# Two-layer graph network: the four table blocks of the 512-wide layer become 44, 45, 47 and 48

## The chip, the cores and the metric

The kernel runs as one program on one core of a Trainium2 chip. The metric is the device time of a run in microseconds, the median of several runs. Of the engines, PE does the matmuls, DVE and ACT elementwise work, POOL the indirect gathers, and SP and ACT issue plain DMAs.

## What is computed

A graph of 6250 nodes and 100000 edges, sorted by destination, passes through an attention layer with batch norms and a feed-forward part, and then three aggregations of the same kind over the same edges:

```python
def _gin_conv(h, src, dst, w, b, eps, n_nodes):
    agg = jax.ops.segment_sum(h[src], dst, num_segments=n_nodes)
    return ((1.0 + eps) * h + agg) @ w + b
...
h = jax.nn.relu(_gin_conv(x, src, dst, w1, b1, eps1, n))   # 256 -> 512
h = jax.nn.relu(_gin_conv(h, src, dst, w2, b2, eps2, n))   # 512 -> 512
return _gin_conv(h, src, dst, w3, b3, eps3, n)             # 512 -> 256
```

The kernel moves the weights around the sum, so that the first and the third aggregation run on rows of 256 values and the second on rows of 512. Each gathered row is `h[src]` of an edge, and the sum goes to the edge's destination.

## The kernel before

The 6250 destination nodes are 50 blocks of 125 (`BLOCKS`, `NB`). The sum of a block is made in one of two ways. A gathered block reads its edge records (up to `RE` = 2176 in a round of `T` = 17 times 128), POOL issues 17 indirect gathers of 128 source rows, DVE makes 17 one-hot matrices, and PE multiplies them. A table block uses a dense count table in DRAM: `adjacency[b]` holds, for each of the 50 source blocks, how many edges run from each source node to each node of block b (128 x 6250 bf16, 1562.5 KB), and PE multiplies table parts with source rows. Edges of a block whose lists overflowed would be gathered in small rounds of `OV` = 32; each table block has at least one such round, on padding.

The stages run one after another, with a barrier between them:

- Edge records and lists are prepared.
- The build (L479 to L616) makes the tables of the blocks in `BUILT`, in rising order. For each of 25 groups of five nodes DVE compares a list with two iotas (L569 `low_hot`, L570 `code_hot`), PE multiplies the two (L615), and 13 evictions per table, on ACT (L587) and from table 12 on one of them on DVE (L567), write a stage buffer that SP stores (L537). From table 12 on POOL does 10 of the 25 `low_hot` comparisons (L522, `low_aside`). Two stage buffers alternate by the table's place d in `BUILT`.
- Attention, batch norms, feed-forward.
- `mixed_layer(0)`, the first 256-wide layer: blocks with b modulo 3 equal to 1 are gathered (L1828), the 33 others (`DENSE_BLOCKS`) use tables, loaded by ACT in parts (L1935).
- `wide_layer(1)`, the 512-wide layer: 46 blocks are gathered (L2258) and four are table blocks. Their sums are kept in four PSUM banks all through the layer; for each of the 50 source blocks, beside the gathers, `source_sums` (L2471) adds that source's contribution to all four. `load_parts` (L2379) fetches the piece of the four tables that belongs to four source blocks, `cast_source` (L2391, L2393) makes it ready, `split_source` (L2321) splits the source rows. The four tables are read with one DMA, through a rearranged view with every second block. `part_loaded` counts these loads. Only in the last eight steps is a block's number a constant; before them it is 2i + s in a loop.
- `mixed_layer(2)`, the last layer, from `rows_last`, which the 512-wide layer has filled by block.

ACT's order in a step of the 512-wide layer: `copy_turned` (the tile `l_zT`, L2361), `store` (L2368), `keep_upper`, then `cast_source` with its loads. The layer begins with six to eight source steps before and around the first gathered block.

Of the kernel before, what the change touches and what calls it, by code (L numbers as in the profile page):

```python
# [57 lines left out]
GATHERED_AT = 1  # L58
TABLED_BLOCKS = [BLOCKS - 2 * TABLED + 1 + 2 * d for d in range(TABLED)]
DENSE_BLOCKS = [b for b in range(BLOCKS) if b % PERIOD != GATHERED_AT]  # L60
BUILT = sorted({*DENSE_BLOCKS, *TABLED_BLOCKS})
DENSE = len(BUILT)
# [35 lines left out]
def build(nc, x, src, dst, Wq, bq, Wk, bk, Wv, bv, Wo, bo, W1, b1, W2, b2, g1, be1, g2, be2,  # L98
# [12 lines left out]
    with ExitStack() as ctx:  # L111
# [1962 lines left out]
        def wide_layer(n, table, w):  # L2074
            k_tiles = w // P
            with ExitStack() as phase:
# [43 lines left out]
                def tabled(s, i):  # L2120

                    return s == 1 and isinstance(i, int) and i >= PAIRS - TABLED

                def record_of(s, i):

                    return (i - (PAIRS - TABLED)) % 2 if isinstance(i, int) and i >= PAIRS - TABLED else s
# [35 lines left out]
                def edge_range(engine, s, i):  # L2162

                    b = 2 * i + s
                    if tabled(s, i):
                        ends = [dense_ends[0:1, e, bass.ds(b, 1)] for e in range(2)]
                    else:
                        ends = [first_edge[0:1, bass.ds(b + e, 1)] for e in range(2)]
                    lo, hi = [engine.value_load(end, min_val=0, max_val=E) for end in ends]
                    return lo, hi  # L2170
# [19 lines left out]
                def _(sp):  # L2190
# [9 lines left out]
                    def load_block(s, i):  # L2200
                        lo, hi = edge_range(sp, s, i)
                        if tabled(s, i):
                            load_few(lo, hi)
                        else:
                            t = record_of(s, i)
                            with sp.Fori(lo, hi, RE) as at:

                                sp.wait_ge(round_gathered[t], count_of(sp, rounds[t]) + 1)
                                sp.dma_start(record[t][:, :, :].rearrange("p j c -> p (j c)"),
                                             edges[bass.ds(at, RE), :].rearrange("(p j) c -> p (j c)", j=T)).then_inc(record_loaded[t], 16)  # L2210
                                sp.reg_add(rounds[t], rounds[t], 1)
                        sp.wait_ge(own_used[s], i + 1)
                        sp.dma_start(own[s][:, :], block_rows(table, 2 * i + s)).then_inc(own_loaded[s], 16)

# [57 lines left out]
                def _(dve):  # L2272
# [9 lines left out]
                    def onehot_few(s, i, lo, hi):  # L2282
                        with dve.Fori(lo, hi, OV) as at:
# [3 lines left out]
                            order.step(dve.tensor_scalar(few_relative[:, :], few_record[:, 1:2].bitcast(F32),  # L2287
                                                         minus_base[0:OV, bass.ds(2 * i + s, 1)], None, ALU.add))
                            dve.tensor_scalar(few_onehot[:, :], column[0:OV, 0:NB], few_relative[:, :], None,
# [4 lines left out]
                    def rounds_of(s, i):  # L2294
# [5 lines left out]
                        with dve.Fori(lo, hi, RE) as at:  # L2300
                            before = count_of(dve, rounds[t])
                            dve.wait_ge(record_loaded[t], before * 16 + 16)
                            order.step(dve.tensor_scalar(relative[t][:, :], record[t][:, :, 1].bitcast(F32),
                                                         minus_base[:, bass.ds(2 * i + s, 1)], None, ALU.add))
                            dve.wait_ge(quarters_used, count_of(dve, seen[t]) * NQ + NQ)
# [35 lines left out]
                    def halve(s, i):  # L2341
# [3 lines left out]
                        dve.sem_inc(upper_cut[s], 1)  # L2345
                        dve.tensor_tensor(rows_last[:, bass.ds(2 * i + s, 1), D:2 * D].rearrange("p o c -> p (o c)"), result[s][:, :],
                                          upper[s][:, :], ALU.subtract).then_inc(lower_ready[s], 1)
# [5 lines left out]
                def _(act):  # L2353
# [10 lines left out]
                    def store(s, i):  # L2364
                        act.wait_ge(product[s], i + 1)
                        act.wait_ge(lower_ready[s], i + 1)
                        act.wait_ge(stored[s], (i + 1) * 16)
                        act.activation(result[s][:, :], product_ps[0:NB, 0:D], ACT.Copy).then_inc(result_ready[s], 1)  # L2368
                        act.wait_ge(result_ready[s], i + 2)
                        act.dma_start(block_rows(table3, 2 * i + s), result[s][:, :]).then_inc(stored[s], 16)  # L2370

                    def keep_upper(s, i):
                        act.wait_ge(upper_cut[s], i + 1)
                        act.activation(rows_last[:, bass.ds(2 * i + s, 1), 0:D].rearrange("p o c -> p (o c)"), upper[s][:, :],
                                       ACT.Copy).then_inc(upper_ready[s], 1)

                    def load_parts(u):
                        width = min(4, BLOCKS - 4 * u) * NB if isinstance(u, int) else 4 * NB
                        act.dma_start(packed[:, :, 0:width],  # L2379
                                      adjacency.rearrange("(d k) p x -> k p d x", k=2)[1, :, PAIRS - TABLED:PAIRS, bass.ds(u * (4 * NB), width)]  # L2380
                                      ).then_inc(part_loaded, 16)

# [3 lines left out]
                    def cast_source(r, a, u):  # L2386

                        v = u * 2 + a // 2
                        act.wait_ge(part_loaded, u * 16 + 16)
                        act.wait_ge(source_used[r], v + 1)  # L2390
# [132 lines left out]
```

## Time and profile before

| | |
|---|---|
| median of 3 runs | 4995.4 us (4991.88 to 4999.53) |
| span of the profiled execution | 4893.1 us |
| around the span, median less span | 102.3 us |
| busy: PE, DVE, ACT, POOL | 78%, 46%, 29%, 55% of the span |
| DMA, mean over the span | 150 GB/s |
| table stores | 35, 1562.5 KB each |
| loads of 500 KB (part loads of the 512-wide layer) | 12, and a smaller thirteenth |

The shares are means over stages that have different limits, so the trace is read by stage: the busy times of a stretch say which engine is never idle, and the timeline of a line that runs once per table or per block gives the pace. An idle time stands in brackets behind an instruction, with what ended it; "issue" means that the trace shows nothing that the engine waited for. SPq and ACTq rows are issues of DMAs on those queues, not their transfers.

### The profile page before, as it was taken

Reading aid. Unit: us, or ns where it says so; the run is one execution under the profiler, and the core shown is the slowest. Engines: PE = TensorE matmul, PEld = TensorE weight load, DVE = VectorE, ACT = ScalarE, POOL = GpSimd, SP = SyncE. Lnnn points to the kernel's source line nnn. Section 1 sums busy time; section 2 is a strip of 40 time slices with the busy share of each in tenths; the row PEclk is TensorE's granted clock in tenths of the full one; section 3 lists DMA queues with packets and bytes.
Section 4 is the critical chain, followed back from the end, with each engine's and each line's share of the span. In section 5 each row is a group of like instructions: output and inputs, shape, how many; then the busy total and the mean of one; then the engine's idle time right before and its main releaser. Section 6 shows DMA issues by size and latency. Waiting matters only on the chain. (4 is left out here: it accounts for less than half of the span.)

```text
span 4893.1 us, 71187 instructions
## 1 busy us (share of the span) xinstructions
PE 3799.9 (78%) x15901; PEld 2488.7 (51%) x15902; DVE 2235.7 (46%) x7891; ACT 1434.7 (29%) x2745; POOL 2679.8 (55%) x4185
## 2 busy tenths in 40 slices
PE   3886645656566556986999999688888888779999
PEld 1233324444444444875677777344444444457777
DVE  6997756767676677345121121222222222222222
ACT  3983222222222222245344444100000000023333
POOL 6781056676766666013544444266666666646664
PEclk9999977777777777985999999799998999889999
DMA  4442233333333333026767666477777776646665
GB/s 138 176 184 92 58 82 92 95 97 96 96 96 96 94 96 86 0 67 179 201 183 206 189 183 185 138 211 210 214 210 206 209 214 206 197 135 208 204 202 178
DMA packets 346846, 734.87 MB, mean 150 GB/s; under 512 B 77407, under 2 KB 171229, under 8 KB 341985
## 3 DMA queue, kind: packets, MB, share of 16 engines
q0 software_dynamic: 176144, 461.72, 33.4%
q10 hardware_dynamic: 100178, 157.63, 10.3%
q1 hardware_dynamic: 70268, 113.00, 6.7%
q14 instruction: 204, 1.67, 0.1%
q8 instruction: 52, 0.85, 0.1%
HBM read 622.28 MB, written 109.84 MB: 150 GB/s over the span
## 5 line engine op out<-in xcount | busy, mean ns | idle before, releaser
L900 POOL DMA_INDIRECT a_gathered<-table,record x850 | 808.2, 951 | 642.6 <-issue 378.5
L2258 POOL DMA_INDIRECT l_gathered<-table,record x782 | 761.0, 973 | 472.1 <-issue 283.4
L2451 PE MATMUL bank<-l_gathered,l_onehot 128*125 128x512 f32 x1564 | 777.0, 652 | 179.1 <-DMA l_gathered<-table,record 110.7
L1828 POOL DMA_INDIRECT l_gathered<-table,record x578 | 546.1, 945 | 463.4 <-PE bank L2036 215.9
L1249 PE MATMUL bank<-a_gathered,a_onehot 128*125 128x264 f32 x1700 | 570.3, 494 | 101.6 <-DVE a_gathered L1053 79.0
L2451 PEld LDWEIGHTS bank<-l_gathered,l_onehot 128*125 128x125 f32 x1564 | 316.3, 207 | 617.3 <-issue 457.6
L1942 ACT ACTIVATE l_part<-l_packed 128x1000 fp32r<-128x1000 bf16 (+1 forms) x396 | 413.3, 1070 | 554.4 <-PE bank L2017 227.1
L1249 PEld LDWEIGHTS bank<-a_gathered,a_onehot 128*125 128x125 f32 x1700 | 393.5, 243 | 203.9 <-issue 76.5
L2017 PE MATMUL bank<-rows_first,l_part 125*125 125x512 f32 x1650 | 406.6, 405 | 29.3 <-ACT l_part L1942 29.2
L2017 PE MATMUL bank<-rows_last,l_part 125*125 125x512 f32 x1650 | 394.5, 398 | 11.3 <-ACT l_part L1942 9.9
L2017 PEld LDWEIGHTS bank<-rows_first,l_part 125*125 125x125 f32 x1650 | 308.4, 187 | 121.2 <-issue 43.9
L2017 PEld LDWEIGHTS bank<-rows_last,l_part 125*125 125x125 f32 x1650 | 304.3, 186 | 89.2 <-issue 12.1
L615 PE MATMUL bank<-d_code_hot,d_low_hot 128*128 128x250 bf16 x875 | 268.7, 385 | 49.7 <-DVE d_code_hot L570 24.2
L587 ACT ACTIVATE d_stage<-bank 128x500 bf16<-128x500 f32 (+1 forms) x432 | 285.5, 726 | 34.9 <-PE bank L615 27.1
L1053 DVE TENSOR_TENSOR a_gathered<-a_gathered,bank 128x1024 f32<-128x1024 f32 x200 | 244.0, 1282 | 40.6 <-ACT bank L1192 27.8
L1892 DVE SCALAR_TENSOR_TENSOR l_work<-rows_first,one_eps,bank 125x256 f32<-125x256 f32 x50 | 24.0, 481 | 497.2 <-PE bank L2044 464.6
L570 DVE TENSOR_SCALAR d_code_hot<-d_code_iota,d_lists 128x250 bf16<-128x250 bf16 x875 | 247.2, 318 | 0.0
L2361 ACT ACTIVATE l_zT<-bank 128x500 f32<-128x500 f32 x50 | 29.3, 587 | 737.0 <-issue 491.7
L2036 PE MATMUL bank<-l_gathered,l_onehot 128*125 128x256 f32 (+1 forms) x867 | 210.7, 400 | 17.1 <-DMA l_gathered<-table,record 17.0
L615 PEld LDWEIGHTS bank<-d_code_hot,d_low_hot 128*128 128x128 bf16 x875 | 91.0, 104 | 226.6 <-DVE d_code_hot L570 79.1
L1264 PE MATMUL bank<-identity_bf,a_onehot_bf 128*128 128x128 bf16 x850 | 82.5, 236 | 144.9 <-ACT a_onehotT L1175 68.5
L569 DVE TENSOR_SCALAR d_low_hot<-d_low_iota,d_lists 128x128 bf16<-128x128 bf16 x645 | 193.7, 303 | 1.2 <-ACT d_lists L577 1.2
(282 smaller groups left out, 5515.3 us busy)
## 6 DMA issues: line engine op xcount, KB each, us to landing
l_packed<-adjacency ACTq DMA_DIRECT2D x265, 250.0 KB
adjacency<-d_stage SPq DMA_DIRECT2D x35, 1562.5 KB
l_packed<-adjacency ACTq DMA_DIRECT2D x132, 281.2 KB
l_gathered<-table,record POOLq DMA_INDIRECT x1360
a_gathered<-table,record POOLq DMA_INDIRECT x850
table<-rows_first POOLq DMA_DIRECT2D x50, 250.0 KB, 3.5
table<-l_work ACTq DMA_DIRECT2D x50, 250.0 KB
l_source_rows<-table ACTq DMA_DIRECT2D x50, 250.0 KB
```

The costliest lines, as they stand in the source:

```text
L570: dve.tensor_scalar(code_hot[g % HOT][:, :], code_iota[:, :], lists[:, c, 1, k:k + 1], None, ALU.is_equal).then_inc(pair_ready, 1)
L587: act.activation(*evict(d, h), ACT.Copy).then_inc(summed_read, 1)
L615: pe.matmul(banks[n % 7][:, (g - g0) * CODES:(g - g0 + 1) * CODES], low_hot[at % HOT][:, :], code_hot[at % HOT][:, :], start=True, stop=Tr ...
L900: pool.indirect_dma_start(out=gathered0[s][:, j * TW:(j + 1) * TW], out_offset=None, in_=table0, in_offset=bass.IndirectOffsetOnAxis(ap=re ...
L1053: dve.tensor_tensor(values[:, j0:j1], values[:, j0:j1], factors[:, j0:j1, :].unsqueeze(3).broadcast_to([P, j1 - j0, HEADS, DH]), ALU.mult) ...
L1249: last = pe.matmul(acc_ps[s][0:NB, 0:TW], onehot[s][:, j, :], rows[:, j, :], start=(j == 0), stop=(j == T - 1), skip_group_check=True)
L1828: pool.indirect_dma_start(out=gathered[g][:, j, :], out_offset=None, in_=table, in_offset=bass.IndirectOffsetOnAxis(ap=record[k.t][:, j, 0 ...
L1942: act.activation(part[r][:, 0:h1 - h0, :].rearrange("p h n -> p (h n)"), packed[r][:, 0:h1 - h0, :].rearrange("p h n -> p (h n)"), ACT.Cop ...
L2017: last = pe.matmul(sum_ps[k.s][0:NB, :], part[r][0:NB, h - h0, :], rows_sb[:, h, :], start=(h == 0), stop=False, skip_group_check=True)
L2036: last = pe.matmul(total, onehot[k.t][:, j, :], gathered[g][:, j, :], start=False, stop=(j == T - 1), skip_group_check=True)
L2258: pool.indirect_dma_start(out=gathered[:, j * w:(j + 1) * w], out_offset=None, in_=table, in_offset=bass.IndirectOffsetOnAxis(ap=record[t] ...
L2451: last = pe.matmul(total[0:NB, 0:w], onehot[t][:, j, :], rows[:, j, :], start=False, stop=(j == T - 1), skip_group_check=True)
```

## The change

`BUILT` becomes `DENSE_BLOCKS`, so that 33 tables are built in place of 35. `TABLED_BLOCKS`, the table blocks of the 512-wide layer, become 44, 45, 47 and 48 in place of 43, 45, 47 and 49. Since the steps at which a table block is taken stay (every second one of the last eight), the last eight steps take the blocks in a new order, `LAST_BLOCKS`; `block_at` maps a step to its block, and own rows, records, stores and `rows_last` go by it. The four table pieces are no longer evenly spaced, so `load_parts` issues four DMAs of a quarter of the size on the same queue, and `cast_source` waits for four times the count.

```diff
 GATHERED_AT = 1
-TABLED_BLOCKS = [BLOCKS - 2 * TABLED + 1 + 2 * d for d in range(TABLED)]
 DENSE_BLOCKS = [b for b in range(BLOCKS) if b % PERIOD != GATHERED_AT]
-BUILT = sorted({*DENSE_BLOCKS, *TABLED_BLOCKS})
+BUILT = DENSE_BLOCKS
+TABLED_BLOCKS = [44, 45, 47, 48]
+LAST_BLOCKS = [42, 44, 43, 45, 46, 47, 49, 48]
...
+                def block_at(s, i):
+
+                    if isinstance(i, int) and 2 * i + s >= BLOCKS - 2 * TABLED:
+                        return LAST_BLOCKS[2 * i + s - (BLOCKS - 2 * TABLED)]
+                    return 2 * i + s
...
-                    b = 2 * i + s
+                    b = block_at(s, i)
...
-                        sp.dma_start(own[s][:, :], block_rows(table, 2 * i + s)).then_inc(own_loaded[s], 16)
+                        sp.dma_start(own[s][:, :], block_rows(table, block_at(s, i))).then_inc(own_loaded[s], 16)
...
                     def load_parts(u):
                         width = min(4, BLOCKS - 4 * u) * NB if isinstance(u, int) else 4 * NB
-                        act.dma_start(packed[:, :, 0:width],
-                                      adjacency.rearrange("(d k) p x -> k p d x", k=2)[1, :, PAIRS - TABLED:PAIRS, bass.ds(u * (4 * NB), width)]
-                                      ).then_inc(part_loaded, 16)
+                        for d, b in enumerate(TABLED_BLOCKS):
+                            act.dma_start(packed[:, d, 0:width], adjacency[b, :, bass.ds(u * (4 * NB), width)]).then_inc(part_loaded, 16)
...
-                        act.wait_ge(part_loaded, u * 16 + 16)
+                        act.wait_ge(part_loaded, (u + 1) * (16 * TABLED))
```

The one-hot comparisons (L2288, L2304), the two writes of `rows_last` (L2346, L2373) and the store (L2370) take `block_at(s, i)` in place of `2 * i + s` in the same way.

## Rows read from the trace of the kernel before

**Rows 1.** stretch of the build: us; busy PE, PEld, DVE, ACT, POOL; PEclk; DMA share, GB/s

```profile
200.00:300.00 100.00, 85.36 (x296) 30.92 (x294) 99.86 (x481) 88.38 (x141) 81.09 (x116) 1.00 0.43 181
```

**Rows 2.** the tile d_stage: ns min/median/max, first and last start; timeline, DVE: start, us

```profile
L567 DVE CAST d_stage<-bank x23: 716/721/752, 201.3 to 392.6; 128x500 bf16<-128x500 f32 x23
...
288.40 0.72 DVE L567 CAST d_stage<-bank 128x500 bf16<-128x500 f32 x1
296.62 0.72 DVE L567 CAST d_stage<-bank 128x500 bf16<-128x500 f32 x1
...
383.78 0.72 DVE L567 CAST d_stage<-bank 128x500 bf16<-128x500 f32 x1
```

**Rows 3.** stores of the tables (tile d_stage), and the timeline of SP after them

```profile
L537 SPq DMA_DIRECT2D adjacency<-d_stage x35: 332/332/357, 84.9 to 396.4; - x35
...
402.94 0.54 SPq L181 DMA_DIRECT2D spare<-identity  x2
```

**Rows 4.** timeline of POOL, 512-wide layer, two block starts: start, us, idle before, releaser

```profile
4102.83 1.01 POOL L2258 DMA_INDIRECT l_gathered<-table,record  x1 [3.56 <-PE bank L2451]
...
4127.76 0.94 POOL L2258 DMA_INDIRECT l_gathered<-table,record  x1 [3.40 <-remote]
```

**Rows 5.** timeline of POOL, the layer's first four block starts and that of block 42

```profile
3098.58 0.96 POOL L2258 DMA_INDIRECT l_gathered<-table,record  x1 [54.17 <-issue]
...
3139.70 0.94 POOL L2258 DMA_INDIRECT l_gathered<-table,record  x1 [19.64 <-PE bank L2451]
...
3177.32 0.97 POOL L2258 DMA_INDIRECT l_gathered<-table,record  x1 [16.53 <-PE bank L2451]
...
3202.14 1.36 POOL L2258 DMA_INDIRECT l_gathered<-table,record  x1 [3.85 <-PE bank L2451]
...
4177.50 0.95 POOL L2258 DMA_INDIRECT l_gathered<-table,record  x1 [3.42 <-PE bank L2451]
```

**Rows 6.** the page's costliest groups: count, busy us, mean ns, idle before

```profile
L570 DVE TENSOR_SCALAR d_code_hot<-d_code_iota,d_lists 128x250 bf16<-128x250 bf16 x875 | 247.2, 318 | 0.0
```

**Rows 7.** groups by line: gathers of the attention stage and small gathers of the 256-wide layers

```profile
L900 POOL DMA_INDIRECT a_gathered<-table,record x850 | 808.2, 951 | 642.6 <-issue 378.5
...
L1810 POOL DMA_INDIRECT l_few_rows<-table,l_few_record x66 | 58.5, 887 | 204.7 <-issue 145.9 <-DMA l_few_record<-edge_records 58.8
```

**Rows 8.** the line L2379, the load of the parts: ns min/median/max

```profile
L2379 ACTq DMA_DIRECT2D l_packed<-adjacency x13: 13/402/700, 3090.8 to 4111.0; - x13
L2379 ACTq FUSED_REGOPS  x8: 15/664/712, 3324.2 to 4017.9; - x8
```

**Rows 9.** timeline of ACT: a load in the loop, and ACT's next work

```profile
3426.16 0.01 ACTq L2379 DMA_DIRECT2D l_packed<-adjacency  x1
3434.75 0.59 ACT L2361 ACTIVATE l_zT<-bank 128x500 f32<-128x500 f32 x1 [10.86 <-issue]
```

**Rows 10.** timeline, start of the 512-wide layer: two part loads and their first casts

```profile
3090.82 0.46 ACTq L2379 DMA_DIRECT2D l_packed<-adjacency  x1
...
3100.98 0.62 ACT L2391 ACTIVATE l_part<-l_packed 128x500 fp32r<-128x500 bf16 x1 [16.46 <-DMA l_packed<-adjacency]
...
3114.68 0.40 ACTq L2379 DMA_DIRECT2D l_packed<-adjacency  x1
...
3127.08 0.62 ACT L2391 ACTIVATE l_part<-l_packed 128x500 fp32r<-128x500 bf16 x1 [12.97 <-DMA l_packed<-adjacency]
```

**Rows 11.** timeline, start of the first 256-wide layer: three loads, and the third's cast

```profile
2308.59 1.34 ACTq L1935 DMA_DIRECT2D l_packed<-adjacency  x3
...
2313.58 1.02 ACT L1942 ACTIVATE l_part<-l_packed 128x1000 fp32r<-128x1000 bf16 x1
```

**Rows 12.** the same columns, two stretches at the start of the 512-wide layer

```profile
3097.00:3099.00 2.00, 0.00 (x0) 0.00 (x0) 0.00 (x0) 0.00 (x0) 0.42 (x1) 0.50 0.33 123
...
3125.00:3127.00 2.00, 0.00 (x0) 0.00 (x0) 0.00 (x0) 0.00 (x0) 0.00 (x0) 0.50 0.11 37
```

**Rows 13.** the chain that ended last, its first piece: start, us, what

```profile
4320.68 1.98 DMA l_few_record<-edge_records
```

More of the change, by code:

```diff
@@ L2287, in onehot_few @@
                             order.step(dve.tensor_scalar(few_relative[:, :], few_record[:, 1:2].bitcast(F32),
-                                                         minus_base[0:OV, bass.ds(2 * i + s, 1)], None, ALU.add))
+                                                         minus_base[0:OV, bass.ds(block_at(s, i), 1)], None, ALU.add))
                             dve.tensor_scalar(few_onehot[:, :], column[0:OV, 0:NB], few_relative[:, :], None,
@@ L2303, in rounds_of @@
                             order.step(dve.tensor_scalar(relative[t][:, :], record[t][:, :, 1].bitcast(F32),
-                                                         minus_base[:, bass.ds(2 * i + s, 1)], None, ALU.add))
+                                                         minus_base[:, bass.ds(block_at(s, i), 1)], None, ALU.add))
                             dve.wait_ge(quarters_used, count_of(dve, seen[t]) * NQ + NQ)
@@ L2345, in halve @@
                         dve.sem_inc(upper_cut[s], 1)
-                        dve.tensor_tensor(rows_last[:, bass.ds(2 * i + s, 1), D:2 * D].rearrange("p o c -> p (o c)"), result[s][:, :],
+                        dve.tensor_tensor(rows_last[:, bass.ds(block_at(s, i), 1), D:2 * D].rearrange("p o c -> p (o c)"), result[s][:, :],
                                           upper[s][:, :], ALU.subtract).then_inc(lower_ready[s], 1)
@@ L2369, in store @@
                         act.wait_ge(result_ready[s], i + 2)
-                        act.dma_start(block_rows(table3, 2 * i + s), result[s][:, :]).then_inc(stored[s], 16)
+                        act.dma_start(block_rows(table3, block_at(s, i)), result[s][:, :]).then_inc(stored[s], 16)
                     def keep_upper(s, i):
                         act.wait_ge(upper_cut[s], i + 1)
-                        act.activation(rows_last[:, bass.ds(2 * i + s, 1), 0:D].rearrange("p o c -> p (o c)"), upper[s][:, :],
+                        act.activation(rows_last[:, bass.ds(block_at(s, i), 1), 0:D].rearrange("p o c -> p (o c)"), upper[s][:, :],
                                        ACT.Copy).then_inc(upper_ready[s], 1)
```

## The prediction

> **What bounds the kernel now.** I read the page's slices first: the program is a chain of stages, each with its own limit, and the change touches two of them, the table build (the first 400 us) and the 512-wide layer (3090 to 4317 us). The question is which engine ends each of the two.
>
> The build. The busy times by stretch show DVE busy 99.86 of 100.00 us between 200 and 300, PE 85.36, ACT 88.38, POOL 81.09, and a DMA share of 0.43 [rows 1]. DVE sets the pace. The copies at L567 come once per table from table 12 on, always at the same place in the table, so they are a clock: 23 of them from 201.3 to 392.6 us [rows 2], 22 intervals, 191.3 / 22 = 8.70 us for a table. The shortest interval is 8.22 us (288.40 to 296.62); the last, 8.81, is one of the many near 8.8. The stage ends in a tail behind DVE: the last store is issued at 396.4, the next stage's first issue comes at 402.94 [rows 3]. These 6.5 us are the landing of one store and the barrier; the number of tables is not in them.
>
> The 512-wide layer. L2258's gathers are its clock: a block starts with the gather that has an idle time of some 3.5 us before it. In the body POOL's starts are evenly spaced: 4102.83 to 4127.76 is 24.93 us [rows 4], and from 3202.14 to 4177.50 there are 39 intervals, 975.36 / 39 = 25.01 us [rows 5]. 17 issues 1.25 us apart are 21.25 of it. So POOL paces, and ACT and PE have room. The start of the layer is the exception: the first block starts are 3098.58, 3139.70, 3177.32, and POOL waits 19.64 and 16.53 us for PE in front of the second and the third [rows 5].
>
> **Term 1, two tables fewer.** BUILT goes from 35 to 33 entries: blocks 43 and 49 are dropped and nothing is added, since 44, 45, 47 and 48 are among the 33 anyway. With a table go 25 comparisons of L570 (875 / 35) [rows 6], 15 or more of L569 and one copy on DVE, and its comparisons on POOL, 25 matmuls, 12 copies on ACT and one store. Only DVE's share is on the path. Both dropped tables are late in the order (places 29 and 34, counted from 0), so the pace from table 12 on applies, and POOL's help goes by the place, which the tables that stay keep. 2 x 8.70 = 17.4 us. Bounds: two of the shortest intervals, 16.4, and somewhat above two of 8.81, 17.8. Taking the lists of chunk 9 is still done once. When DVE ends earlier, ACT and PE are late next; they were idle 12 and 15% of the time behind DVE, so they end as much earlier, and the store's tail follows. The later stages only start earlier.
>
> **Term 2, the order of the last eight blocks.** The 512-wide layer takes 42, 44, 43, 45, 46, 47, 49, 48 in place of 42 to 49. Four are still gathered and four still come from tables, at the same positions. A gathered block of over 2176 edges would need a second round of 17 gathers; the attention stage gathers all 50 blocks with 850 = 50 x 17 issues [rows 7], so 43 and 49 need one round each. A table block whose lists overflowed would need some 60 small rounds; the two 256-wide layers do 66 = 2 x 33 small gathers for their 33 table blocks each [rows 7], one per block, so the tables of 44, 45, 47 and 48 are whole. Block 49 reads some padding records, with the same number of issues. Cost 0.
>
> **Term 3, the load of the parts.** L2379 issued one DMA per four source blocks, 13 in all; now it issues four, 39 more, all on ACT's queue. An issue there takes 0.40 us in the median; in the loop, up to 0.70, with up to 0.71 of register work before it [rows 8]. So 3 x 0.40 = 1.2 us at least and 3 x 1.41 = 4.2 us at most come ahead of ACT's next work, `l_zT`. The shortest time from a load to that is 8.6 us (3426.16 to 3434.75) [rows 9]; 4.2 us are covered, and POOL's pace is a second cover behind ACT. Queued behind the issues are also, once, the loads of weights at L2405 and L2406, needed when the first block's sum is complete. The bytes and their pieces (1000 bytes each, 512 of them) stay.
>
> Not covered is the start of the layer. The first part load is issued at 3090.82 and the cast that waits for it starts at 3100.98; the second at 3114.68, with its cast at 3127.08 [rows 10]; a third follows. Each stands in the chain to POOL's second or third block. Bound above by the issues alone: 3 x 1.2 = 3.6 us. Bound below: in the 256-wide layer three loads of 281 KB are issued from 2308.59 on within 1.34 us, and the cast of the third starts at 2313.58, 5.0 us after the first issue [rows 11]. If the four small ones landed in 5.0 us, the first two loads would gain 10.2 - 5.0 = 5.2 and 12.4 - 5.0 = 7.4 us, some 12 together. I take 0, going by the DMA rows: before these casts the DMA share is 0.33 (3097 to 3099) and 0.11 (3125 to 3127) [rows 12], so a few engines work off a backlog while the others stand idle, and an issue that comes 1.2 us later joins the same backlog. The loads of `source_rows`, 125 rows each, go out on the same queue just before the part.
>
> The Trainium skill, page "DMA: Bandwidth & Descriptors", section "Why a DMA increments its semaphore by 16 and not by 1", says that a DMA from ACT or SP runs on the largest number of engines up to 16 that divides its outer size: 5 for 125 rows, 16 for 128. The trace agrees, 5 / 16 being 0.31 beside the 0.33. By that rule the part runs on 16 engines in one piece or in four, and waits behind the source rows on five of them, which gives 0 as well; the loads without a backlog [rows 11] would give the gain of 12.
>
> **Sum.** The profiled execution's span is 4893.1 us; the runs' median is 4995.4, so 102.3 us lie around the span, taken as unchanged. 4893.1 - 17.4 + 0 + 0 = 4875.7 us of span, and with 102.3 that is 4978.0 us.
>
> **Rivals.**
> 1. The four small loads land sooner at the start of the 512-wide layer, by up to 12 us: 4966 to 4973. For it the fast landing of [rows 11], against it the share of 0.33.
> 2. The four pay their latency one after another where nothing covers it. The smallest load of the critical chain takes 1.98 us [rows 13]; three more of these at three exposed loads are 17.8 us, and the gain is gone: 4982 to 4996. Against it, the three loads of [rows 11] overlap.
> 3. Slower than before: ACT becomes late in the body of the 512-wide layer. Eight loads in the loop cost up to 4.2 us each and five outside it 1.2, 39.6 us if nothing is covered: 4978.0 + 39.6 = 5017.6. It decides only once the added issues of a load take over 8.6 us, the shortest cover [rows 9]. Against it, POOL's period is 24.93 us where a load falls into it (the last, at 4111), and 25.01 over all.
> 4. The build does not shrink, because its end is set by something that doesn't count tables, such as the fetch of the lists: 4985 to 4995. Against it, DVE has no idle time in the stretch of [rows 1].
>
> On rival 2 the skill's same page, section "Anatomy of one DMA — SWDGE (gpsimd) path", puts the fixed cost of a DMA at about 2.0 us; in series that would be an estimated 3 x 3 x 2.0 = 18 us, and the overlapping loads of this trace speak against adding it up.
>
> **How the numbers follow.** Forecast 0.72, its own range 4973 to 4983 (1 us for term 1, 3.6 for term 3, and some 4 for the median, the runs before lying from 4991.88 to 4999.53). Rival 1 0.08, rival 2 0.12, rival 3 0.04, rival 4 0.04. The range 4967 to 4985 takes in the forecast, nearly all of rival 1 and the near part of rival 2. About 0.2%, 10 us, is what a measurement of this kernel can tell from no change, so faster means below 4985.4: 0.72 + 0.08 + 0.05 of rival 2 = 0.85. Slower is rival 3, 0.04; the rest, 0.11, is within 0.2%.
>
> **What would show it.** Term 1: 33 stores, 21 copies at L567, still 8.7 us apart, and the next stage's first issue near 385.5 in place of 402.94. Term 2: 782 gathers at L2258, 850 and 66 as before. Term 3: 52 issues at the part load's line, POOL's period still 25.0 us, and 111.3 us from the first part load to POOL's fourth block start (3090.82 to 3202.14); a longer distance is rival 2, a shorter one rival 1, a period above 25.1 is rival 3. The prediction would be wrong at its root if a stage that the diff doesn't name changed its length by more than a few us.

## The result, and the profile after

The changed kernel takes 4971.9 us (median of 7 runs, 4951.5 to 4984.0), the kernel before 4995.4 us beside it (median of 7, 4982.1 to 5006.5). The ratio is 0.995, with a 95% interval of 0.9931 to 0.9968: faster by 16 to 34 us. The forecast was 4978.0. The measured time lies just outside the forecast's own 4973 to 4983, in the part of the stated range (4967 to 4985) that was taken in for rival 1.

The head of the changed kernel's page:

```profile
span 4949.9 us, 70982 instructions
```

The span is 57 us longer than that of before, 4893.1, though the median is 23.5 us shorter. The profiled execution of after took 4951.5 us, its span and 1.6 us. If as little lies around the span of before, that execution took about 4895 us, far below its own median and below the shortest of the seven runs, 4982.1. So two single spans of this kernel say nothing of 20 us, and the comparison has to go by stage. Stages are told apart by the first issue or the first gather of the next one:

| us | before | after | difference |
|---|---|---|---|
| build, to the next stage's first issue | 402.9 | 386.3 | -16.7 |
| from there to the first gather of the attention stage | 238.2 | 240.1 | +1.9 |
| attention gathers | 1297.8 | 1339.1 | +41.3 |
| batch norms, feed-forward and residual | 368.6 | 373.6 | +5.0 |
| first 256-wide layer | 781.9 | 783.3 | +1.4 |
| 512-wide layer | 1227.5 | 1232.5 | +5.0 |
| last layer | 576.1 | 594.9 | +18.8 |

The build did what was forecast. The largest difference is in a stage that the diff does not touch. The tile d_stage of after (ns min/median/max, first and last start), and the timeline of SP where the build ends:

```profile
L538 SPq DMA_DIRECT2D adjacency<-d_stage x33: 332/332/357, 83.8 to 379.8; - x33
...
L568 DVE CAST d_stage<-bank x21: 719/722/743, 200.2 to 376.0; 128x500 bf16<-128x500 f32 x21
...
386.28 0.54 SPq L182 DMA_DIRECT2D spare<-identity  x2
```

There are 33 stores in place of 35 and 21 copies in place of 23 [rows 2, 3]. The tail from the last store's issue to the next stage, 379.8 to 386.28, is 6.5 us as before. The copies are (376.0 - 200.2) / 20 = 8.79 us apart, a little more than the 8.70 of before. The same stretch of the build as in [rows 1] (us; busy PE, PEld, DVE, ACT, POOL; clock; DMA share; GB/s):

```profile
200.00:300.00 100.00, 84.07 (x290) 30.36 (x289) 99.86 (x473) 88.77 (x140) 80.77 (x114) 1.00 0.42 177
```

DVE is as full as before, with 473 instructions in place of 481: the same steps, a little slower.

The 512-wide layer, timeline of ACT: the first two loads of the parts with their casts, and two in the loop, a short one and the longest, with ACT's next work:

```profile
3124.04 1.98 ACTq L2387 DMA_DIRECT2D l_packed<-adjacency  x4
...
3134.28 0.62 ACT L2397 ACTIVATE l_part<-l_packed 128x500 fp32r<-128x500 bf16 x1 [16.40 <-DMA l_packed<-adjacency]
...
3148.40 1.80 ACTq L2387 DMA_DIRECT2D l_packed<-adjacency  x4
...
3159.18 0.62 ACT L2397 ACTIVATE l_part<-l_packed 128x500 fp32r<-128x500 bf16 x1 [11.35 <-DMA l_packed<-adjacency]
...
3361.41 1.49 ACTq L2387 DMA_DIRECT2D l_packed<-adjacency  x4
3372.80 0.59 ACT L2368 ACTIVATE l_zT<-bank 128x500 f32<-128x500 f32 x1 [13.69 <-issue]
...
3755.86 10.66 ACTq L2387 DMA_DIRECT2D l_packed<-adjacency  x4
3774.08 0.59 ACT L2368 ACTIVATE l_zT<-bank 128x500 f32<-128x500 f32 x1 [19.18 <-PE bank L2486]
```

Four issues take 1.4 to 2.5 us in eight of the 13 loads and 4.4 to 10.7 us in the other five, all of them in the loop. From the first issue to the cast it is 10.2 and 10.8 us, where one DMA took 10.2 and 12.4 [rows 10]. In the loop ACT's next work comes 11.4 us after the first issue of the short load and 18.2 us after that of the longest, where it waits for PE. POOL's block starts:

```profile
3131.89 0.96 POOL L2265 DMA_INDIRECT l_gathered<-table,record  x1 [54.18 <-issue]
...
3236.03 1.36 POOL L2265 DMA_INDIRECT l_gathered<-table,record  x1 [4.17 <-PE bank L2457]
...
4226.03 0.94 POOL L2265 DMA_INDIRECT l_gathered<-table,record  x1 [3.70 <-PE bank L2457]
```

From the first part load to the fourth block start it is 3236.03 - 3124.04 = 112.0 us (before 111.3). The 39 intervals to 4226.03 are 25.38 us each (before 25.01 [rows 5]). That is above the 25.1 which was to stand for a late ACT. The interval that holds the longest load, 3743.5 to 3768.9, is 25.4 us as well, so the length of the issues does not make the difference; what does is not shown. Over 39 intervals it is 14 us, yet the layer is only 5.0 us longer, since from the last gather of a whole block to the next stage it is 24.7 us in place of 36.8.

### The profile page after: what moved, and what is told of

Read it like the earlier page. It is cut to its first block and busy times, and to the rows that moved or that the text cites. A ratio compares the mean times of both kernels' runs of the same rounds, so it can differ in the third digit from the quotient of the medians.

```text
span 4949.9 us, 70982 instructions
## 1 busy us (share of the span) xinstructions
PE 3790.0 (77%) x15851; PEld 2476.6 (50%) x15852; DVE 2219.8 (45%) x7809; ACT 1423.3 (29%) x2721; POOL 2673.2 (54%) x4165
## 3 DMA queue, kind: packets, MB, share of 16 engines
q10 hardware_dynamic: 100802, 157.63, 10.2%
## 5 line engine op out<-in xcount | busy, mean ns | idle before, releaser
L2457 PE MATMUL bank<-l_gathered,l_onehot 128*125 128x512 f32 x1564 | 781.9, 654 | 196.2 <-DMA l_gathered<-table,record 117.0
L2018 PE MATMUL bank<-rows_last,l_part 125*125 125x512 f32 x1650 | 402.9, 402 | 29.5 <-ACT l_part L1943 19.5
L616 PE MATMUL bank<-d_code_hot,d_low_hot 128*128 128x250 bf16 x825 | 254.4, 385 | 48.5 <-DVE d_code_hot L571 24.0
L588 ACT ACTIVATE d_stage<-bank 128x500 bf16<-128x500 f32 (+1 forms) x408 | 271.4, 725 | 33.5 <-PE bank L616 23.8
L571 DVE TENSOR_SCALAR d_code_hot<-d_code_iota,d_lists 128x250 bf16<-128x250 bf16 x825 | 234.7, 320 | 0.0
L2328 DVE TENSOR_SCALAR l_source_cut<-l_source_rows 125x512 int32<-125x512 int32 x50 | 21.7, 434 | 374.1 <-remote 318.6
```

What stands on the lines that cost most here:

```text
L571: dve.tensor_scalar(code_hot[g % HOT][:, :], code_iota[:, :], lists[:, c, 1, k:k + 1], None, ALU.is_equal).then_inc(pair_ready, 1)
L588: act.activation(*evict(d, h), ACT.Copy).then_inc(summed_read, 1)
L616: pe.matmul(banks[n % 7][:, (g - g0) * CODES:(g - g0 + 1) * CODES], low_hot[at % HOT][:, :], code_hot[at % HOT][:, :], start=True, stop=Tr ...
L2018: last = pe.matmul(sum_ps[k.s][0:NB, :], part[r][0:NB, h - h0, :], rows_sb[:, h, :], start=(h == 0), stop=False, skip_group_check=True)
L2457: last = pe.matmul(total[0:NB, 0:w], onehot[t][:, j, :], rows[:, j, :], start=False, stop=(j == T - 1), skip_group_check=True)
```

## The experiments

**Theory.** The gain is DVE's time for two tables, 17.4 us, and the new order and the small loads are free. **Rivals.** The loads help or hurt at the start of the 512-wide layer; ACT is late in its body; or the build gains less and some other stage gives the rest. The runs that follow were made on three chips: b on number 3, c on number 0, d on number 14. The runs of the kernel before beside them have medians of 4696.8, 4698.5 and 4697.0 us, in place of the 4995 above. The record has no number for the chip of that first measurement; that it was another one is inferred from the time. Ratios are to the runs of the kernel before on the same chip.

### b1_before_again and b2_after_again

Both kernels again, unchanged, each with a profile: whether the stages that the diff does not name differ.

> The kernel before, word for word, once more. Its profile of before has a span of 4893.1 us, 102 us under the median of its runs, while every run of the changed kernel has a span 1.6 us under its time. Theory A (the stages that the change does not name differ from execution to execution, or from chip to chip, not from kernel to kernel): the span is near 4990 us, ratio 1.000, the attention gathers take more than the 1298 us of before, and POOL's period in the 512-wide layer more than 25.01 us, near the 25.38 of after. Theory B (the change itself lengthens the stages it does not name, by 42 us in the attention stage and 19 in the last layer): this kernel's attention gathers take 1298 us and its period is 25.0 us again.

> The changed kernel, word for word. Theory A: ratio 0.995 to 0.997 to the kernel before, and the lengths of the attention stage and of the last layer equal to those of the kernel before on this chip within 3 us. Theory B: the same ratio, but the attention stage 40 us longer than that of the kernel before on this chip, which would leave room for a saving that the build does not explain.

The kernel before takes 4697.9 us (11 runs; ratio to its own runs beside it 1.0006, 0.9997 to 1.0015), the changed one 4683.4 us (7 runs; ratio 0.9972, 0.9961 to 0.9983). Gathers of the attention stage, first of before, then of after (ns min/median/max, first and last start):

```profile
L900 POOL DMA_INDIRECT a_gathered<-table,record x850: 944/945/1217, 636.8 to 1895.4; - x170
```

```profile
L901 POOL DMA_INDIRECT a_gathered<-table,record x850: 944/945/1112, 623.5 to 1882.7; - x170
```

1895.4 - 636.8 = 1258.6 us and 1882.7 - 623.5 = 1259.2: the 41 us are gone, and in all eleven profiles of the later chips, of whatever kernel, this stage takes 1257.3 to 1261.1 us. Theory A is right in that the two kernels do not differ here, but its numbers missed: it expected a span near 4990, over 1298 us in this stage and a period of POOL above 25.01, and they are 4690.3, 1258.6 and 21.59. The 41 us go with the first measurement; neither kernel was run again there. The builds end here, first before, then after (timeline of SP):

```profile
400.08 0.54 SPq L181 DMA_DIRECT2D spare<-identity  x2
```

```profile
385.37 0.54 SPq L182 DMA_DIRECT2D spare<-identity  x2
```

This is 14.7 us. From here on the start of the 512-wide layer is measured from the layer's first issue, not from the first part load. The 512-wide layer's first issue to POOL's fourth block start is 100.0 us in the one and 100.2 in the other. POOL's period in the body is 21.59 and 21.68 us. Neither the start nor the body has changed.

### b3_four_loads

The kernel before, with the part loaded by four DMAs; the tables and the order stay.

```diff
-                        act.dma_start(packed[:, :, 0:width],
-                                      adjacency.rearrange("(d k) p x -> k p d x", k=2)[1, :, PAIRS - TABLED:PAIRS, bass.ds(u * (4 * NB), width)]
-                                      ).then_inc(part_loaded, 16)
+                        for d, b in enumerate(TABLED_BLOCKS):
+                            act.dma_start(packed[:, d, 0:width], adjacency[b, :, bass.ds(u * (4 * NB), width)]).then_inc(part_loaded, 16)
...
-                        act.wait_ge(part_loaded, u * 16 + 16)
+                        act.wait_ge(part_loaded, (u + 1) * (16 * TABLED))
```

> The kernel before with one part of the change alone: the parts of the four tables (43, 45, 47, 49, all 35 built) are loaded with four DMAs in place of one, and the cast waits for four times the count. My theory: ratio 1.000 (0.999 to 1.001), period of POOL in the 512-wide layer equal to that of the kernel before on this chip within 0.05 us. Rival 2 (four loads pay their latency in series where nothing covers it): up to 17.8 us more, ratio up to 1.0036. Rival of the period: the split adds 0.3 us to each of 44 blocks, 13 us, ratio 1.0027.

4696.4 us (11 runs), ratio 1.0000 (0.9991 to 1.0009). The start takes 100.0 us and the build ends at 402.24. The loads alone change nothing: this is against both rivals that placed up to 12 us of gain or 18 of loss at the start of the layer.

### b4_tables35

The changed kernel, with the two tables built that nothing reads.

```diff
-BUILT = DENSE_BLOCKS
+BUILT = sorted({*DENSE_BLOCKS, 43, 49})
```

> The changed kernel, but with 35 tables built (43 and 49 again, which nothing reads). Undoes the build's part alone; the order of the last eight blocks and the four loads stay. My theory: 17.4 us above the changed kernel, so ratio 1.000 to the kernel before, and 35 stores of tables with the build ending at 402.9 us. If the order of the blocks or the loads carry the gain, the ratio stays at 0.995.

4698.2 us (11 runs), ratio 1.0002 (0.9993 to 1.0011), the build's end at 402.89. With the order and the loads of the changed kernel but all 35 tables the gain is gone. So it lies in the tables alone, and the new order costs nothing that these runs can tell.

### c1_tables41

The changed kernel with eight more tables, so that the price of one is read from a long lever.

```diff
-BUILT = DENSE_BLOCKS
+BUILT = sorted({*DENSE_BLOCKS, 28, 31, 34, 37, 40, 43, 46, 49})
```

> The changed kernel with eight tables more, 41 built (28, 31, 34, 37, 40, 43, 46 and 49 besides the 33; nothing reads the added ones). My theory, 8.70 us per late table: 8 x 8.70 = 69.6 us above the changed kernel, so 55 us above the kernel before if the changed one is 14.5 below it, ratio 1.0117, and a build ending at 385.8 + 69.6 = 455 us. If two tables are worth only the 14.5 us by which the medians of the changed kernel and of the one with 35 tables differ, 7.25 us per table: 58 us above the changed kernel, 43 above the kernel before, ratio 1.0093, build ending at 444 us.

4756.9 us (5 runs), ratio 1.0128 (1.0109 to 1.0147). The copies of DVE and the end of the build (the tile d_stage and the timeline of SP):

```profile
L568 DVE CAST d_stage<-bank x29: 716/723/752, 201.1 to 448.4; 128x500 bf16<-128x500 f32 x29
...
458.84 0.53 SPq L182 DMA_DIRECT2D spare<-identity  x2
```

(448.4 - 201.1) / 28 = 8.83 us for a table. The build ends 458.84 - 386.0 = 72.8 us after the mean end of the builds with 33 tables. That is 9.1 us for each of the eight, above the 8.70 expected (455 us) and somewhat above the 8.83, since the other tables were slower here too: 28 x 8.83 is 72.2 us more than the 20 x 8.75 of the kernels with 33. Build and time grow together: 4756.9 is 73.5 us above b2, and the ratios differ by 0.0156, which is 73 us. So the number of tables sets the stage's end, which leaves nothing of the rival by which it does not shrink.

### c2_sixteen_loads and c3_two_loads

The changed kernel with each piece in four DMAs of 32 partitions, 16 per load, and with two DMAs of two blocks each per load.

```diff
-                            act.dma_start(packed[:, d, 0:width], adjacency[b, :, bass.ds(u * (4 * NB), width)]).then_inc(part_loaded, 16)
+                            for p0 in range(0, P, 32):
+                                act.dma_start(packed[p0:p0 + 32, d, 0:width],
+                                              adjacency[b, p0:p0 + 32, bass.ds(u * (4 * NB), width)]).then_inc(part_loaded, 16)
```

```diff
-                        for d, b in enumerate(TABLED_BLOCKS):
-                            act.dma_start(packed[:, d, 0:width], adjacency[b, :, bass.ds(u * (4 * NB), width)]).then_inc(part_loaded, 16)
+                        for d in (0, 2):
+                            b = TABLED_BLOCKS[d]
+                            act.dma_start(packed[:, d:d + 2, 0:width],
+                                          adjacency[b:b + 2, :, bass.ds(u * (4 * NB), width)].rearrange("c p x -> p c x")).then_inc(part_loaded, 16)
```

The wait counts 16 for each DMA, as before (`16 * 4 * TABLED` and `16 * (TABLED // 2)`).

> The changed kernel with each of the four loads of a part cut again into four of 32 partitions: 16 issues per four source blocks, 208 in all. My theory: the loop is covered while the issues ahead of ACT's next work take under 8.6 us; 12 further issues at 0.36 to 1.41 us are 4 to 17 us per load, 13 loads. With the median of 0.36 it stays covered and costs 0 to 5 us (ratio to the kernel before 0.997 to 0.998); with 1.41 it is past the point, and each of the eight loads of the loop costs some 12 us less what POOL's own slack swallows, up to 90 us (ratio up to 1.016). Rival 2 (latencies in series at the three exposed loads): 3 x 12 x 2.0 = 71 us more, all of it between the layer's start and the fourth block start.

> The changed kernel with two DMAs per four source blocks in place of four: blocks 44 and 45 in one, 47 and 48 in the other. My theory: nothing to win, ratio 0.997 as the changed kernel, start of the 512-wide layer to the fourth block start 100 us as with four loads and with one. Rival 2: 1 to 9 us faster than the changed kernel, at the start of the layer.

4686.3 us (8 runs, ratio 0.9974, 0.9963 to 0.9984) and 4685.5 us (10 runs, 0.9973, 0.9964 to 0.9983). A load in the body with sixteen issues, timeline of ACT:

```profile
3236.03 7.96 ACTq L2388 DMA_DIRECT2D l_packed<-adjacency  x16
3253.38 0.59 ACT L2368 ACTIVATE l_zT<-bank 128x500 f32<-128x500 f32 x1 [17.05 <-PE bank L2488]
```

The issues take 7.96 us, some four times those of the changed kernel on these chips, and ACT's next work still comes when PE is done, 17.35 us after the first issue. POOL's period in the body is 21.55 us and the start takes 100.9 us. ACT's slack has room for sixteen issues, so it has room for four. Where it ends was not reached, and nothing here tests it under the conditions of the first measurement.

### c4_help5 and d3_help12

The changed kernel with POOL doing 5 and 12 of the 25 `low_hot` comparisons of a table in place of 10: what the pace of the build hangs on.

```diff
-                return at // GB >= POOL_FROM and at % GB % 5 in (1, 3)
+                return at // GB >= POOL_FROM and at % GB % 5 == 1
```

```diff
-                return at // GB >= POOL_FROM and at % GB % 5 in (1, 3)
+                return at // GB >= POOL_FROM and (at % GB % 5 in (1, 3) or at % GB in (5, 15))
```

> The changed kernel with POOL taking 5 of the 25 low comparisons of a table from table 12 on, in place of 10; DVE makes the others. Tests that DVE paces the build. A table of tables 0 to 11, 25 low and 25 code comparisons without a copy on DVE, takes 8.96 us (8 stores in 71.65 us), one with help 8.70 with a copy of some 0.6, so a low comparison more is worth about 0.09 us on DVE: 21 tables x 5 x 0.09 = 9.5 us more, build ending at 395 us in place of 385.8, ratio to the kernel before 0.999. If DVE were not the pace (ACT, PE or the stores), the build ends at 385.8 and the ratio stays 0.997.

> The changed kernel with POOL taking 12 of the 25 low comparisons of a table from table 12 on, in place of 10. With 5 in place of 10 the build was 9.7 us longer (395.74 against a mean of 386.0), 0.092 us per comparison. My theory: 21 x 2 x 0.092 = 3.9 us off, build ending at 382 us, ratio 0.0008 below the changed kernel's. Rival: POOL, 12 x 0.73 = 8.8 us of a table's 8.8, becomes the pace, and the build ends at 386 or later.

With 5 the build ends at 395.74, 9.7 us later than the mean of 386.0 in the builds with 10, and the time is 4699.6 us (11 runs, ratio 1.0006, 0.9997 to 1.0015). With 12 it ends at 376.05, 9.9 us earlier, and the time is 4674.3 us (5 runs, ratio 0.9953, 0.9940 to 0.9967). With 5 the ratio is above the 0.999 that was expected: the time is some 14 us above that of c2 and c3 on the same chip, 4 us more than the build accounts for; 2.3 of them lie between the build and the attention stage (241.3 us where c2 and c3 have 239.0 in the mean). The ends of the build (timeline of SP), with 5 and with 12, and the same stretch of it:

```profile
395.74 0.54 SPq L182 DMA_DIRECT2D spare<-identity  x2
```

```profile
376.05 0.54 SPq L182 DMA_DIRECT2D spare<-identity  x2
```

```profile
200.00:300.00 100.00, 84.64 (x277) 29.12 (x276) 99.90 (x505) 86.11 (x133) 38.76 (x55) 1.00 0.41 170
```

```profile
200.00:300.00 100.00, 88.31 (x313) 30.99 (x312) 99.86 (x483) 91.55 (x150) 100.00 (x148) 0.75 0.47 197
```

DVE is full in both, as with 10, and taking comparisons from it makes the build shorter. In d3_help12 POOL is full as well, and the granted clock has a mean of 0.75: it fell in the middle of the stretch. Two parts before the fall and one after it, in the same columns:

```profile
230.00:240.00 10.00, 8.98 (x33) 3.10 (x32) 10.00 (x51) 9.41 (x16) 10.00 (x14) 1.00 0.58 242
240.00:250.00 10.00, 7.71 (x33) 2.95 (x31) 9.96 (x50) 9.02 (x16) 10.00 (x16) 0.99 0.53 222
250.00:260.00 10.00, 8.66 (x32) 2.87 (x32) 10.00 (x48) 8.70 (x15) 10.00 (x16) 0.50 0.43 180
```

PE was busy for 8.98 and 7.71 of 10 us at the upper level (1.00, 2.4 GHz) before it went to the lower one (0.50, 1.2 GHz). It does 33 matmuls in each of the first two and 32 in the third: PE does not set the pace even at half its clock. With POOL full too, these rows don't tell whether DVE or POOL sets the pace with 12.

For two comparisons fewer, -3.9 us was expected; -9.9 came. The distances between copies tell why. With 5 they are 9.1 us, or 9.6 where DVE also takes a new chunk of lists. With 12 they are 8.0 to 8.2 (two are 8.5), or 8.4 to 8.7 with a chunk. With 10 there are stretches of 8.22 and stretches of 8.83. The 8.22 fits what the comparisons cost, (9.10 - 8.22) / 5 = 0.18 us each; and twice that less is 7.9, near the 8.0 to 8.1 with 12. So the 8.83 is an excess of 0.6 us per table that shows with 10 and hardly with 5 or 12, and the kernel with 12 gains the excess as well as the comparisons.

d3_help12 beats both kernels: by 22.7 us the one before and by 7 us the changed one on the same chip (d1).

### d1_after_third and d2_before_third

Both kernels once more, for the scatter of the stages.

> The changed kernel once more, beside other runs of the kernel before. The first comparison gave a median 23.5 us lower (ratio 0.995, 0.9931 to 0.9968) where the kernel before took 4995 us, the second 13.4 us lower (0.9972) where it took 4697. My theory: the build gives 14 to 18 us wherever it runs, so the ratio is 0.9965 to 0.997, and the first figure is the same gain with a wider scatter. Rival: the gain depends on the chip, 23 us where the gathers wait for their landings (period of POOL 25.0 us) and 14 where they don't (21.6 us).

> The kernel before, word for word, for its profile beside the run of the changed kernel on the same chip. Every stage after the build within 4 us of the changed kernel's, the build 14 to 18 us longer, the tables at L567 either 8.2 or 8.8 us apart.

The changed kernel takes 4681.5 us (9 runs, ratio 0.9972, 0.9962 to 0.9982), the kernel before 4698.6 us in its one run here (the 13 runs beside it: median 4697.0). Every stage after the build is within the 4 us that was expected; the build differs by 18.2 us, just over the 14 to 18. With these there are five profiles of each kind, by the number of tables:

| us | 35 tables (before, b1, b3, b4, d2) | 33 tables (after, b2, c2, c3, d1) |
|---|---|---|
| end of the build | 402.9, 400.1, 402.2, 402.9, 404.0; mean 402.4 | 386.3, 385.4, 384.0, 388.3, 385.8; mean 386.0 |
| copy to copy, mean | 8.70, 8.61, 8.70, 8.73, 8.79; mean 8.70 | 8.79, 8.75, 8.65, 8.81, 8.76; mean 8.75 |
| to the attention stage's first gather | 238.2, 236.7, 237.2, 237.1, 236.6 | 240.1, 238.1, 239.4, 238.6, 238.7 |

The 512-wide layer takes 1066.6, 1066.9 and 1066.4 us with the old order (b1, b3, d2) and 1070.6, 1069.6, 1067.9, 1066.9, 1063.9 and 1067.1 with the new one and four loads (b2, b4, c1, c4, d1, d3): means of 1066.6 and 1067.7, and the new order's own scatter is 6.7 us.

## Why the prediction was right, point by point

**The bound of the build** was read rightly as DVE, with one reserve. It is full at 5, 10 and 12 comparisons of POOL, and the build follows what is left on DVE (395.7, 386.0, 376.1 us). But with 10 a table of 8.8 us is more than DVE's own steps: a new chunk of lists takes DVE 0.45 us and makes a table of 8.22 one of 8.64, while tables of 8.83 stay at 8.83 with it.

**Term 1, 17.4 us,** measures 402.4 - 386.0 = 16.4 us (16.5 before rounding) over five profiles each. The mean pace was 8.75 in place of 8.70 in the shorter builds, which gives back 20 x 0.05 = 1.0 us, and that is nearly all that is missing. This 0.05 is within the scatter of the single profiles (8.61 to 8.79 and 8.65 to 8.81), so it need not come from the change. The error is in the size of a term whose mechanism holds. It was hidden because the pace is no constant. The intervals of the copies come in two sizes. Here in b1_before_again (timeline of DVE), two of 8.85 and 8.73 us and then one of 8.22:

```profile
200.41 0.72 DVE L567 CAST d_stage<-bank 128x500 bf16<-128x500 f32 x1
...
209.26 0.72 DVE L567 CAST d_stage<-bank 128x500 bf16<-128x500 f32 x1
...
217.99 0.72 DVE L567 CAST d_stage<-bank 128x500 bf16<-128x500 f32 x1
...
226.21 0.72 DVE L567 CAST d_stage<-bank 128x500 bf16<-128x500 f32 x1
```

Of 22 intervals 2 to 8 are below 8.5 us with 35 tables, and of 20 intervals 1 to 6 with 33. They come one to four together, and each such run begins directly behind an interval of 8.6 to 8.8 us in which DVE takes a chunk of lists, as here (217.99 - 209.26); but not every chunk begins one. One execution's end of the build is a draw from these: single differences between a build with 35 tables and one with 33 reach from 11.8 to 20.0 us. The prediction's bounds, 16.4 to 17.8, took the shortest and the long interval of one profile as limits for a difference of two executions. For that they are too narrow.

**Term 2, the order, 0.** b4_tables35 has the new order and 35 tables, at 1.0002 of before. Right.

**Term 3, the loads, 0.** b3_four_loads has them alone, at 1.0000. The cost of the issues was not always in its bounds, 1.2 to 4.2 us for the three added ones: four take 1.8 to 3.2 us on the later chips, but 4.4 to 10.7 us in five of the 13 loads of the profile of after, the longest beyond even the 8.6 us that were to decide. It counted one step of register work for each DMA; there are two on ACT's queue, and in that profile the steps take some 0.7 us with pauses between them. What saved the term is the cover, 18.2 us at the longest load, where the prediction had taken the shortest, 8.6. The guess that the small loads join the backlog which the one load met fits the 10.2 us to the first cast in both kernels. In any case the size of the loads cannot have mattered much, since 2, 4 and 16 per load give starts of 100.3, 100.2 and 100.9 us.

**What ends the body of the 512-wide layer** was read wrongly. The prediction said that POOL paces there. POOL's waits from 3200 to 4100, first in the profile of before, then in b1_before_again (us in total, times, longest):

```profile
POOL l_gathered L2258 <- issue: 174.6, 573, 0.3
POOL l_gathered L2258 <- PE bank L2451: 72.5, 23, 3.9
POOL l_gathered L2258 <- remote: 55.9, 16, 3.8
```

```profile
POOL l_gathered L2258 <- issue: 200.3, 631, 4.7
POOL l_gathered L2258 <- PE bank L2451: 16.8, 55, 0.3
```

In the first measurement POOL stood still for some 3.5 us in front of every block, 128 us in these 900. An engine that waits once per block does not set the pace; by these rows it was something behind the buffers, and what is not shown. On the later chips the pauses are nearly gone, and the period is 21.6 us, close to 17 issues of 1.25. The prediction had the 3.5 us in its rows [rows 4, 5] and passed over them. It did no harm here: on chip 3 the period is 21.59 us with one load (b1) and 21.57 with four (b3). It did weaken one argument: the second cover, "POOL's pace", behind ACT's issues was not there in the first measurement.

**The sum.** "102.3 us lie around the span" was false. In the later runs, and in those of the changed kernel, 1.6 to 2.0 us do (4951.5 and 4949.9 in the profile of after); so the rest was most likely that the profiled execution of before was quicker than the median, by some 100 us, and why is not known. The forecast does not hang on it, since it is the median less 17.4. A reader who had taken 4875.7 for the next profile's span would have met 4949.9.

**The rivals.** Small loads land sooner, or in series: no (b3, c2, c3). A late ACT: not with 16 issues either (c2). The build does not shrink: no (c1, b4). All four answers rest on the later chips. The 4971.9 us fall where rival 1 had put its time (4966 to 4973), but no run shows its mechanism.

**The criterion for a wrong root** was badly chosen. "A stage that the diff doesn't name changed its length by more than a few us" came true, with +41 us in the attention stage, while the theory holds. Both kernels, run again, have 1258.6 and 1259.2 us there. On the later chips the attention stage would have kept to a few us, but the 512-wide layer lies anywhere in 1062.0 to 1070.6 us and the last one in 578.3 to 587.5. One stage of one execution against one of another is no test of a few us there, and none at all in the first measurement; the same goes for the criterion of 25.1 us for POOL's period.

**What stays open.** First, the stretch between the build and the first gather is longer by 1.8 us in the mean with 33 tables (five against five; 236.6 to 238.2 against 238.1 to 240.1), without a cause that the runs show. c4_help5 has 241.3, d3_help12 237.4 and c1_tables41 238.0, so it doesn't go by the number of tables alone. The gain is then 16.4 - 1.8 = 14.6 us, and the medians on the later chips give 13.4 (b2) and 15.5 (d1), 12.2 and 13.1 with c2 and c3. Second, in the first measurement it is 23.5 us, with an interval of 16 to 34. Whether the gain is larger there or the 14.6 fell just outside by chance wasn't settled, as no later run took 4995 us before. That 4971.9 came out as near to 4978.0 as it did is in part luck: of the 23.5 us the build explains 16 to 17, and the end of the 512-wide layer, 12 us shorter in one pair of profiles, is a rival that was not tested there.

## What to carry to other kernels

Find an instruction that runs once per unit of work on the engine that is never idle; its distance times the units removed is the forecast, and a kernel with many units more measures the price with less scatter than the change itself does (c1_tables41). Take the distance from several executions or allow for its scatter, and subtract from the median, never from the span of one profile. Before an engine is called the bound of a loop, its idle time per turn has to be nil: a steady period with a wait in it is somebody else's.

## What the runs showed of the hardware

- One kernel took 4995 us in the first measurement and 4697 to 4699 us on three other chips. The build (402.9 and 400.1) and the first 256-wide layer (781.9 and 783.1) are alike. The attention stage (1297.8 and 1258.6) and the 512-wide layer (1227.5 and 1066.6) hold the difference between the two profiles, that is, the stages that gather on POOL all through. The stretch 3200 to 4100, before and b1_before_again:

```profile
3200.00:4100.00 900.00, 760.10 (x2017) 375.89 (x2016) 251.71 (x864) 86.04 (x177) 598.04 (x612) 0.92 0.71 210
```

```profile
3200.00:4100.00 900.00, 809.49 (x2328) 407.79 (x2326) 288.70 (x978) 99.73 (x207) 666.93 (x692) 0.99 0.78 237
```

  The later chip (number 3) does 2328 matmuls where the first measurement has 2017, at a granted clock of 0.99 in place of 0.92, and moves 237 GB/s in place of 210. Register steps of the queues differ more than anything else. The line that steers SP's loads in the 512-wide layer (L2213 of the changed kernel), in after and in d1_after_third (ns min/median/max):

```profile
L2213 SPq FUSED_REGOPS  x46: 4/702/1414, 3124.0 to 4306.9; - x46
```

```profile
L2213 SPq FUSED_REGOPS  x46: 47/47/47, 3036.2 to 4042.1; - x46
```

  It is the same in before (L2206: 4/699/1397) and b1_before_again (47/47/47). Steps fifteen times as long on the queue that loads every block's records are a candidate for the slower body. Which of these is cause was not tried.
- The same 41 DVE instructions of a table take 8.2 us in some tables and 8.8 in others. In b1_before_again a `low_hot` comparison in a slow table and one in a fast table (timeline of DVE):

```profile
203.56 0.39 DVE L569 TENSOR_SCALAR d_low_hot<-d_low_iota,d_lists 128x128 bf16<-128x128 bf16 x1
203.87 0.47 DVE L570 TENSOR_SCALAR d_code_hot<-d_code_iota,d_lists 128x250 bf16<-128x250 bf16 x2
...
219.53 0.24 DVE L569 TENSOR_SCALAR d_low_hot<-d_low_iota,d_lists 128x128 bf16<-128x128 bf16 x1
219.70 0.47 DVE L570 TENSOR_SCALAR d_code_hot<-d_code_iota,d_lists 128x250 bf16<-128x250 bf16 x2
```

  The next start comes 0.31 us later in the one and 0.17 in the other; a slow table has several such places. All of them lie where POOL is in a comparison of its own: between 200 and 360 us the next start comes over 0.25 us later 64 times in c1_tables41 and 36 times in b1_before_again, each time with POOL busy, and never in the 54 and 56 comparisons that began with POOL idle. With 5 of the comparisons on POOL there are 23 such places, one or so per table, and with 12 only two. So DVE and POOL seem to get in each other's way at certain offsets; no run tested it, and why 12 does not show it is open.
- The part loads of 500 KB can be cut into 2, 4 or 16 DMAs each at no cost in time that these runs show, as long as ACT has the slack. On the later chips four issues on ACT take 1.8 to 3.2 us and sixteen 7.5 to 8.4; in the profile of after four take 1.4 to 10.7.
